# One 128-partition turn of the head maxima, four row transfers, and a step of two in the plain products' weights

## The reference

```python
ctx = X @ We.T                                   # 16 columns
influence = einsum('bqe,bke->bqk', ctx, ctx)
Q, K, V = heads(Wq), heads(Wk), heads(Wv)        # 16 heads of 8
scores = einsum('bhqd,bhkd->bhqk', Q, K) * SCALE + 0.1 * influence[:, None]
attn = softmax(scores, axis=-1)
out = einsum('bhqk,bhkd->bhqd', attn, V) ... @ Wo.T
```

## Time and profile before

| what | value |
|---|---|
| median of 3 runs | 726.56 us |
| lowest run | 724.34 us |
| span of the profiled execution | 724.1 us |
| TensorE matmul busy | 663.7 us, 92% |
| VectorE busy | 650.1 us, 90% |
| ACT busy | 531.9 us, 73% |
| GpSimd busy | 514.5 us, 71% |
| SyncE's transfers from the stack's `mT` source | 128 of 2.0 KB |
| VectorE transposes | 256, 51.3 us |

### The profile page before, as it was taken

How to read it: one execution, slowest core, us unless ns; L and a number is a source line. 1 busy time by engine, 2 the same in 40 slices (tenths; PEclk the granted TensorE clock), 3 DMA queues, 4 the chain that set the end, 5 groups by cost and what they waited for, 6 DMA issues and landing times.

```text
span 724.1 us, 25378 instructions
## 1 busy us (share of the span) xinstructions
PE 663.7 (92%) x8084; PEld 448.1 (62%) x8084; DVE 650.1 (90%) x1177; ACT 531.9 (73%) x1123; POOL 514.5 (71%) x613
## 2 busy tenths in 40 slices
PE   0377899999999999799999999999999999999996
PEld 0263445555555555599999999999455555555554
DVE  8989989999999999699999999999899999898991
ACT  2593388888888888667767767777787787787885
POOL 8680477777677656077777887787688888888782
PEclk9986799999999999999999999999999999999999
DMA  8859466776676676633333333332577777877652
GB/s 249 307 170 336 135 166 169 182 200 161 175 209 173 174 191 174 160 76 96 93 96 93 97 96 90 97 92 75 142 155 179 191 178 183 173 178 187 176 122 67
DMA packets 124919, 113.37 MB, mean 157 GB/s; under 512 B 16416, under 2 KB 112416, under 8 KB 124832
## 3 DMA queue, kind: packets, MB, share of 16 engines
q1 hardware_dynamic: 115600, 90.63, 47.7%
q0 software_dynamic: 8192, 16.86, 9.6%
q10 hardware_dynamic: 1040, 4.76, 1.8%
HBM read 64.72 MB, written 47.19 MB: 155 GB/s over the span
## 4 chain that ended last, share of the span: by engine, by line
PE 65%; DVE 13%; SPq 8%; DMA 6%; issue 5%; ACT 2%; ACTq 0%; DVEq 0%
PE bank L1266 13%; PE mx L1255 13%; PE bank L1135 12%; PE bank L1113 11%; PE mx L1147 7%; DVE mx L961 6%; DMA stack<-qk_dram 6%; PE bank L1033 2%; PE bank L1247 2%; PE bank L1195 2%; DVE A L796 2%; SPq L331 2%; PE bank L1157 1%; ACT A L715 1%; PE bank L1164 1%
## 5 line engine op out<-in xcount | busy, mean ns | idle before, releaser
L715 ACT ACTIVATE A<-bank 128x512 f32<-128x512 f32 x502 | 278.2, 597 | 63.8 <-PE bank L1135 55.8
L961 DVE TENSOR_REDUCE mx<-mx 128x4 f16<-128x1024 f32 x256 | 302.7, 1205 | 19.1 <-PE mx L1147 14.7
L1135 PE MATMUL bank<-stack 113*128 113x256 f16 x1004 | 170.4, 276 | 1.3 <-ACT A L715 0.8
L761 ACT ACTIVATE rows<-mx,b 128x256 f32<-128x256 f32 x284 | 120.1, 480 | 57.7 <-PE mx L1255 55.3
L556 POOL DMA_INDIRECT slots_x<-rows,pos x128 | 123.6, 966 | 51.8 <-PE bank L1135 32.0
L570 POOL TENSOR_SCALAR rows<-rows,slot_p 128x128 f32<-128x128 f32 x142 | 124.6, 887 | 43.9 <-DVE rows L1009 43.9
L607 POOL DMA_INDIRECT rows<-slots_y,pos x128 | 121.5, 950 | 37.5 <-issue 17.3
L1113 PE MATMUL bank<-A,V 128*32 128x256 f32 x2048 | 137.9, 387 | 1.7 <-ACT A L715 1.6
L1135 PEld LDWEIGHTS bank<-stack 113*128 113x128 f16 x1004 | 72.4, 97 | 89.4 <-ACT A L715 53.8
L1266 PE MATMUL bank<-w,rows 128*128 x1704 | 107.7, 219 | 0.6 <-DVE rows L1003 0.6
L1003 DVE TENSOR_TENSOR rows<-rows 128x512 f16<-128x512 f32 x142 | 101.4, 714 | 4.9
(11 more groups left out here) (145 smaller groups left out, 684.9 us busy)
## 6 DMA issues: line engine op xcount, KB each, us to landing
stack<-ctx_rest SPq DMA_DIRECT2D x64, 256.0 KB
stack<-qk_dram SPq DMA_DIRECT2D x128, 96.0 KB
rows<-slots_x SPq DMA_DIRECT2D x71, 129.0 KB, 2.3
slots_y<-rows SPq DMA_DIRECT2D x71, 128.0 KB, 1.8
qk_dram<-hi_qk SPq DMA_DIRECT2D x64, 128.0 KB
stack<-ctx_high SPq DMA_DIRECT2D x128, 64.0 KB
slots_x<-A ACTq DMA_DIRECT2D x1, 4644.0 KB, 20.3
w_stage<-in_w SPq DMA_DIRECT2D x8, 512.0 KB
```

What stands on the lines that cost most here:

```text
L715: act.activation(A[:, n % NA, :, :].rearrange("p h s -> p (h s)"), scores(k, n)[:, :], ACT.Exp, scale=SCALE).then_inc(s_xp, 1)
L761: act.activation(h32[r % 2][:, fc, :], bank[fc][:, 0:SLOT], ACT.Gelu_apprx_tanh, bias=b1[:, bass.ds(e + fc, 1)], scale=1 / FS).then_inc(s_ ...
L961: dve.tensor_reduce(mx[:, a, 8 * qt:8 * qt + 8].rearrange("q (i e w) -> q i e w", i=2, e=2)[:, :, g % 2], MX[u % 2][:, :].rearrange("q (i ...
L1135: mm = pe.matmul(scores(k, n)[:, i * S:(i + 1) * S], stack[0:SHIFT + 1, par, h, 1, c * P:(c + 1) * P], stack[0:SHIFT + 1, par, h, 0, :], s ...
```

## The change

`mx` gets 32 columns for each query tile, `mT` 128 partitions. The four transposes become one over 128 partitions and 64 columns, which writes the two tiles' columns in turn. The two tiles now hold every second query: tile 0 the even ones, tile 1 the odd ones, so the plain products take their weights from the stack with a step of two. A 32-partition block of `mT` then holds 64 neighbouring queries of all heads of the half, and the row is sent by four transfers, one for each block. The counts that are waited for change from 32 to 64 for each use. The clearing of `mx` at the start (GpSimd) covers 128 columns rather than 64.

```diff
-        mx = sb("mx", [P, 2, 32], F16)
-        mT = sb("mT", [32, 2, 2, P], F16)
+        mx = sb("mx", [P, 2, 2, 32], F16)
+        mT = sb("mT", [P, 2, 2, 64], F16)
...
-                for c in range(2):
-                    sp.dma_start(stack[SHIFT:SHIFT + 1, par1, 8 * a:8 * a + 8, 0, c * P:(c + 1) * P], mT[8 * c:8 * c + 8, par1, a, :]).then_inc(s_mr[par1][a], 16)
+                for i in range(4):
+                    sp.dma_start(stack[SHIFT:SHIFT + 1, par1, 8 * a:8 * a + 8, 0, 64 * i:64 * i + 64], mT[32 * i:32 * i + 8, par1, a, :]).then_inc(s_mr[par1][a], 16)
...
-            pool.memset(mx[:, :, :], 0.0).then_inc(s_post, 1)
+            pool.memset(mx[:, :, :, :], 0.0).then_inc(s_post, 1)
...
-                        dve.tensor_reduce(mx[:, a, 8 * qt:8 * qt + 8]...
+                        dve.tensor_reduce(mx[:, a, qt, 0:8]...
                         if u in (3, 7):
...
-                                dve.wait_ge(s_mr[par1][a], 32 * half1)
-                            for i in range(4):
-                                ins = dve.transpose(mT[:, par1, a, 32 * i:32 * i + 32], mx[32 * i:32 * i + 32, a, :])
-                            ins.then_inc(s_mt, 1)
+                                dve.wait_ge(s_mr[par1][a], 64 * half1)
+                            dve.transpose(mT[:, par1, a, :].rearrange("p (r c) -> p c r", c=2), mx[:, a, :, :]).then_inc(s_mt, 1)
...
-                            pe.wait_ge(s_mr[par][u // 4], 32 * (half + 1))
+                            pe.wait_ge(s_mr[par][u // 4], 64 * (half + 1))
...
-  pe.matmul(MX[v % 2]..., stack[r0:r1, par1, h, 0, v % 2 * P:(v % 2 + 1) * P], stack[r0:r1, par1, h, 1, :], ...
+  pe.matmul(MX[v % 2]..., stack[r0:r1, par1, h, 0, v % 2::2], stack[r0:r1, par1, h, 1, :], ...
```

More of the change, by code:

```diff
@@ L960, in attend @@
                         dve.wait_ge(s_mx, 8 * b1_ + u + 1)
-                        dve.tensor_reduce(mx[:, a, 8 * qt:8 * qt + 8].rearrange("q (i e w) -> q i e w", i=2, e=2)[:, :, g % 2], MX[u % 2][:, :].rearrange("q (i w k) -> q i w k", i=2, w=2), AX.X, ALU.max).then_inc(s_red, 1)
+                        dve.tensor_reduce(mx[:, a, qt, 0:8].rearrange("q (i e w) -> q i e w", i=2, e=2)[:, :, g % 2], MX[u % 2][:, :].rearrange("q (i w k) -> q i w k", i=2, w=2), AX.X, ALU.max).then_inc(s_red, 1)
                         if u in (3, 7):
@@ L1146, in plain @@
                                 h = 8 * (v // 4) + 4 * i + 2 * (v // 2 % 2) + p
-                                mm = pe.matmul(MX[v % 2][:, (2 * i + p) * S:(2 * i + p + 1) * S], stack[r0:r1, par1, h, 0, v % 2 * P:(v % 2 + 1) * P], stack[r0:r1, par1, h, 1, :],
+                                mm = pe.matmul(MX[v % 2][:, (2 * i + p) * S:(2 * i + p + 1) * S], stack[r0:r1, par1, h, 0, v % 2::2], stack[r0:r1, par1, h, 1, :],
                                                start=True, stop=True)
```

## The result

The changed kernel takes 755.76 us, the median of 4 runs (753.37 to 758.61), against 726.57 us for the kernel before in the same comparison (4 runs, 724.34 to 726.74). The ratio is 1.0409, 95% interval 1.0375 to 1.0442: slower by 29 us. Forecast were 736.5 us, range 727 to 752. The direction was right, the size a third of the real one. The profiled execution has a span of 751.6 us at a mean granted clock of 0.976.

A forecast was written before the change was run, and what follows sets the result against it. TensorE, VectorE's maxima and the stack loads were taken to carry a step together. SyncE full +9.1, rows late +1.8, VectorE's relief -1.0: +9.9 on the 724.1 us span, 734.0, median 2.5 over: 736.5 us, range 727 to 752.

The forecast's parts named there:

- the weights for nothing: TensorE's plain products: weights read with a step of two cost nothing; up to +54 us as a rival, chance 0.06.
- SyncE as the bound of the second stage: Eleven full second-stage steps: SyncE's issues sum to 14.2 us against 13.37 us a step, +9.1 us.
- waits of L1133 on `mT`: Sign of being right: in the first stage, new waits of TensorE's shifted products on the transposed maxima (there called L1135).
- The rival of hidden issues: Smaller transfers issue in 0.35 us, so VectorE's relief shows: about -10 us, 716.5 us; chance 0.11.
- Third, half 1's: Second half's load 1.36 us later with room, its row's end 2.72 us later: within 0.1, or up to 0.5 us a step.
- the next t: Start of SyncE's issues in the following step, when the element's shifted products are half done; delays were to be absorbed by then.
- Second, half 0's row: First half's row lands about when TensorE asks for it: step 13.45 us, 0.1 us more, +1.8 us over eighteen steps.
- its overhead: SyncE's register work and loop branch before the next step, taken as 0.3 us on top of 13.93 us.
- sum of 12.7 us: SyncE's total for a step without the stores, from which the first stage was held not bound by SyncE.
- landing, not issuing: Rows land 2.5 us after the last issue: first-stage steps 14.3 us, +13 us on top, 750 us; chance 0.11.
- The relief: VectorE time freed by the single transpose: -1.0 us where SyncE doesn't hold the step; 10 us if nothing else takes its place.
- The waits of L1145 on it: Sign of being right: plain products' waits on VectorE gone (there called L1147; 23.2 us for weight loads, 4.2 for matmuls).

The follow-up runs named there:

- e14_four: The kernel before with four transfers of 8 x 128 B for each half instead of two of 8 x 256 B, nothing else changed; 754.51 us, ratio 1.0411.
- e18_only0: The kernel before with four transfers of 8 x 128 B in the first half of each step, its two in the second; 736.8 us, ratio 1.015.
- e17_nostore: The changed kernel with the second stage's result stores all issued after its last step; 759.36 us, ratio 1.0453.
- e10_eight: The changed kernel with each transfer of maxima cut in two, eight of 8 x 64 B for each half; 902.41 us, ratio 1.2446.
- e15_behind: The kernel before with two idle transfers more for each half, issued behind the write (half 0) or the row (half 1); 751.72 us, ratio 1.0328.
- e16_turn: The changed kernel with two transfers of 8 x 256 B for each half, half of the maxima not sent; 722.83 us, ratio 0.9954.
- e13_after: The changed kernel again, unaltered, as base line on a chip of the faster kind; 755.93 us, ratio 1.0426.
- e19_only1: The kernel before with four transfers of 8 x 128 B in the second half of each step, its two in the first; 729.48 us, ratio 1.0046.

## Why the prediction was wrong

**What held.** The issue's price (2.72 us a step forecast, 2.73 found: 2.71 + 2.74 less two times 1.36), the transpose's 0.25 us, the weights for nothing (the Trainium skill, "TensorE: Matmul & The Clock Gate", "Weight-path perf modes", and the trace agree: 94 ns with a step of two), SyncE as the bound of the second stage, waits of L1133 on `mT`. The rival of hidden issues is out: e14_four, 28.8 us for 128 added issues. The Trainium skill calls the time to initiate a transfer "usually small relative to the DMA itself" ("DMA: Bandwidth & Descriptors", "Issuing engines are not separate DMA queues"); here an issue took 0.64 us and the landing followed 1.0 to 2.9 us behind the last one, so the trace disagrees.

**The step that failed** is the one called "Third, half 1's": "The load is wanted half a step later and has room", a delay "being made up by the next t". From the earlier trace rows SyncE "doesn't wait at all" ahead of its second load; I wrote that down and counted only its idle time over the whole step. But an interval in which an engine has no idle time passes every added issue on. The second load is issued 1.4 us later (6.04 to 7.48), and by the landings in the two traces it reaches the stack about 0.2 us ahead of its first product in the second stage, where it had about 1.3 us (medians). TensorE can make up a part: in e18_only0 the second interval shrinks by 1.0 us (7.39 to 6.37), so a step loses 0.37 us. In the changed kernel that interval is itself full of the other 1.36 us of issues, shrinks by 0.35 only, and a step loses 1.1: with both halves SyncE has nothing left over the whole step, and its sum is the bound, which was forecast. That is why the halves together cost more than one by one. e17_nostore says the same from the other side: with the stores gone the second interval is 6.41, as in e18_only0, and a step is still 0.3 us over that of before.

The larger part of the miss is the first stage's (9.4 of 17.6 us), and there a second step failed too, the one called "Second, half 0's row": it takes the first half's load to land at 5.94 us, as before.

**The two sizes.** Second stage: 14.2 us forecast, 14.49 found, 12.3 for 9.1 us. SyncE is full there as forecast, and the 0.3 us for its overhead was too little: ahead of a step's first load it idles 0.30 and 0.67 us by turns, what e10_eight shows where SyncE hardly ever waits.

First stage: 0.1 us a step forecast, 0.77 found, 10.8 us for 1.4. There SyncE's sum over a step isn't the bound: e10_eight's 18.49 less its added 5.44 gives 13.05 us. The full first interval is longer: 6.07 us before, 7.46 after, and the second gave back 0.53 (7.31 to 6.78; steps 1 to 12). But the loss isn't spread evenly. Some issues and one wait of the first stage after (L407 loads expert weights, 512 KB):
```profile
116.41 0.37 SPq L327 DMA_DIRECT2D stack<-ctx_rest  x1
...
147.25 0.36 SPq L327 DMA_DIRECT2D stack<-ctx_rest  x1
...
159.84 0.37 SPq L407 DMA_DIRECT2D w_stage<-in_w  x1
160.54 0.34 SPq L327 DMA_DIRECT2D stack<-ctx_rest  x1
...
168.46 0.61 PE L1145 MATMUL mx<-stack 64*128 64x256 f16 x8 [2.14 <-DMA stack<-qk_dram]
...
177.34 0.36 SPq L327 DMA_DIRECT2D stack<-ctx_rest  x1
```
The two steps from 116.41 and the one from 160.54 take 47.6 us, 7.6 us more than three steps of before; the other eleven lose 0.29 us each. In the step from 160.54 the first half's products start 7.92 us after the load's first issue, not 5.94 + 0.14. A load of weights had gone out 0.70 us ahead of it. Before, such a load went out well ahead:
```profile
205.38 0.36 SPq L407 DMA_DIRECT2D w_stage<-in_w  x1
208.67 0.34 SPq L327 DMA_DIRECT2D stack<-ctx_rest  x1
```
In the six such places the distance is 0.65 to 1.05 us (2.76 to 3.34 before), and the stack load lands 6.1 to 7.8 us after its first issue (5.6 to 6.7 before; by the landings in the two traces). TensorE's matmuls wait 5.4 us for the row in this stage and 5.1 for stack loads (none and 2.0 before). Of the 5.1 us only 0.4 go to the second half's load; 4.7 go to the first half's, 4.0 of them behind a load of weights. So a part of the first stage's loss seems to come from added issues that push the stack load against the load of weights, which the prediction's sum of 12.7 us had left out. That is read from traces and not tested: no run without the big load was made on these chips.

The rival "landing, not issuing" named 14.3 us a step, near what came, but its reason was half 0's row, 2.5 us after its last issue. That row landed after 1.88 us (median of steps 3 to 12), after 2.1 to 3.1 us behind a load of weights and 1.0 to 1.9 us in the other steps; and e15_behind lost as much with fewer waits for it.

**The relief.** Forecast -1.0 us, and up to 10 if nothing else were late; e16_turn: -2.9. In the changed kernel VectorE's reduce waits 42.8 us for the plain products, 14.7 before: what VectorE saves it idles. The waits of L1145 on it, which I said would be gone, are 19.1 us still, 27.4 before.

**Clock.** 0.982 before, 0.976 after. Part of the difference stands in the long steps of the first stage, where the kernel before has no such fall:
```profile
132.60:136.00 3.40, 3.40 (x24) 1.55 (x25) 1.19 (x2) 1.50 (x4) 0.97 (x1) 0.50 1.01 278
170.10:173.50 3.40, 3.40 (x25) 1.72 (x25) 1.57 (x3) 1.96 (x5) 1.37 (x2) 0.51 0.59 176
```
The granted clock (third number from the end) is at its lower level, 1.2 GHz, in both stretches. Before they began, TensorE had idled for landings: 0.44 and 0.90 us at 131.00 and 132.52, 2.14 us at 168.46. Such a fall costs at most half its length, 3.4 us for both (an estimate from these rows), and TensorE's busy time rose by 2.1 us. In e13_after, e14_four, e15_behind, e17_nostore and e19_only1 too each fall in this stage stands in a step of 15.7 to 17.0 us. So a late landing seems to cost more than its wait, and one such step moves the mean of fourteen by 0.2 us.

**Open.** Why the same issues hardly cost on three of six chips isn't settled: there the step is longer for another reason, which the profile calls remote, and SyncE has idle time; what those signals wait for no run shows. How the 4.4 us at the stages' ends arise wasn't tried, nor what the first stage would lose without the load of weights. e19_only1's 0.29 us a step in the first stage is one step of 16.81 us, with a stack load 0.93 us behind a load of weights, a wait of 2.10 us for it and the lower clock after; the other thirteen take 13.39 us each.

## What to carry to other kernels

Count the issues of a queue interval by interval between the points at which it really waits, not over the whole step: where it shows no idle time an added issue moves everything behind it, even in an engine that idles for a sixth of the step. Cutting a small transfer in two doubles its price on the issuing engine; it is worth it only for work on an engine that is the bound, and 90% busy isn't proof of that. Look too at what the later issues then stand next to: a large load that used to go out well ahead may now go out just before a load that is waited for. And an edit's cost belongs to the chip's own pace: measured where the step is longer for another reason, this one looked like 0.6%.

## What the runs showed of the hardware

- An issue of an SBUF to SBUF transfer of 8 pieces occupied SyncE for 0.64 us whether a piece had 256, 128 or 64 B, where transfers from DRAM into the stack took 0.35 to 0.38 us (L327, L331).
- A row of maxima landed 1.0 to 2.9 us after its last issue (medians of the kernels and stages on the chips of 726 us): in the first stage's half 0, 2.53 us for a group of two issues, 1.88 for four and 1.07 for eight (steps 3 to 12). So part of a longer group's price came back. Within the changed kernel it was 2.1 to 3.1 us in steps behind a load of 512 KB, 1.0 to 1.9 in the others.
- The same program took 756 us on some chips and 807 on another, and the kernel before 727 and 803: an edit's cost on one chip isn't its cost on another.
- One 128x64 transpose of f16 took 252 ns, four of 32x32 took 200 ns each.
